# Two semaphores for the dispatched rows of even and odd images, and a wait for the image two back

## What is computed

```
x = x + mixer(ln(x))
t = ln(x) as 8192 tokens
logits = t @ gate_w + gate_b
choice = the best (layer 0) or the two best (layers 1 to 3) of the experts
y = sum over the chosen experts e of  weight[e] * expert_e(t)
x = x + y
```

## Time and profile before

| what | value |
|---|---|
| median of 3 runs | 2364.84 us (2357.2 to 2367.01) |
| profiled execution: its own time, its span | 2363.5 us, 2361.8 us |
| busy share of the span | TensorE 74%, VectorE 66%, ScalarE 50%, GpSimd 42% |
| GpSimd's returns (line 1212) | 488 of 987 ns, 481.8 us busy |
| GpSimd's sends (line 795) | 448, about 0.96 us each, 445.0 us busy |
| DMA | 153.81 MB, 65 GB/s on average |
| granted clock of TensorE | 0.87 of full speed on average |

### The profile page before, as it was taken

How to read it: one execution, slowest core, us unless ns; L and a number is a source line. 1 busy time by engine, 2 the same in 40 slices (tenths; PEclk the granted TensorE clock), 3 DMA queues, 4 the chain that set the end, 5 groups by cost and what they waited for, 6 DMA issues and landing times. The chain is left out here.

```text
span 2361.8 us, 46309 instructions
## 1 busy us (share of the span) xinstructions
PE 1751.2 (74%) x10964; PEld 1380.4 (58%) x10981; DVE 1549.3 (66%) x4683; ACT 1176.6 (50%) x2637; POOL 980.9 (42%) x969
## 2 busy tenths in 40 slices
PE   1488665895388887989971477779918999988992
PEld 1133554895243443989971244657717777687992
DVE  6898686676677777635537677645665677754554
ACT  2445774895233332757752233446726444454661
POOL 0000133453004343655544066677740255466662
PEclk9799666998699999999995687789959999999996
DMA  2002002222201011232223112133343010123326
GB/s 73 1 0 69 16 25 55 55 77 88 82 2 35 22 33 54 64 85 69 68 75 115 36 46 75 60 89 104 90 142 109 19 34 31 50 70 97 92 78 218
DMA packets 183551, 153.81 MB, mean 65 GB/s; under 512 B 40290, under 2 KB 162818, under 8 KB 183358
## 3 DMA queue, kind: packets, MB, share of 16 engines
q1 hardware_dynamic: 153406, 92.37, 14.5%
q0 software_dynamic: 29952, 59.26, 7.4%
HBM read 85.33 MB, written 68.79 MB: 65 GB/s over the span
## 5 line engine op out<-in xcount | busy, mean ns | idle before, releaser
L1212 POOL DMA_INDIRECT returned<-rows_second_choice x488 | 481.8, 987 | 329.5 <-DVE rows_second_choice L1143 119.3
L1011 PE MATMUL psum<-rows_first_choice 128*128 128x128 f32 x3360 | 473.2, 282 | 19.1 <-ACT rows_first_choice L1060 14.7
L1021 PE MATMUL psum<-expert_weights,rows_first_choice 128*128 x2784 | 428.3, 290 | 61.6 <-ACT rows_first_choice L1077 21.8
L1011 PEld LDWEIGHTS psum<-rows_first_choice 128*128 128x128 f32 x3360 | 431.8, 199 | 21.1 <-issue 15.1
L1021 PEld LDWEIGHTS psum<-expert_weights,rows_first_choice 128*128 128x128 f32 x2784 | 362.8, 198 | 99.2 <-issue 93.0
L795 POOL DMA_INDIRECT dispatched<-rows_first_choice,slot x192 | 191.6, 998 | 525.2 <-DVE rows_second_choice L695 375.9
L1077 ACT ACTIVATE rows_first_choice<-psum,bias_columns 128x128 f32<-128x128 f32 x1104 | 323.4, 368 | 171.4 <-PE psum L1011 154.3
L795 POOL DMA_INDIRECT dispatched<-rows_second_choice,slot x192 | 191.5, 998 | 58.5 <-issue 58.2
L1118 DVE COPY rows_first_choice<-expert_weights 128x512 f32 (+1 forms) x272 | 105.5, 388 | 147.4 <-PE psum L1011 122.1
L326 PE MATMUL psum<-identity,rows_first_choice 128*128 128x128 f32 x256 | 41.2, 320 | 202.8 <-DVE rows_first_choice L313 190.8
L1143 DVE SCALAR_TENSOR_TENSOR rows_second_choice<-psum,rows_second_choice,rows_first_choice 128x128 f32<-128x128 f32 x344 | 119.4, 347 | 103.4 <-PE psum L1021 101.3
(11 more groups left out here) (369 smaller groups left out, 3272.9 us busy)
## 6 DMA issues: line engine op xcount, KB each, us to landing
rows_second_choice<-dispatched SPq DMA_DIRECT2D x488, 65.0 KB
expert_weights<-returned SPq DMA_DIRECT2D x12, 1024.0 KB, 10.4
rows_second_choice<-returned SPq DMA_DIRECT2D x8, 1024.0 KB, 10.7
returned<-rows_second_choice POOLq DMA_INDIRECT x488
expert_weights<-in_L_ffn_w SPq DMA_DIRECT2D x3, 2048.0 KB, 8.3
residual<-in_x SPq DMA_DIRECT2D x8, 512.0 KB, 7.2
rows_first_choice<-returned SPq DMA_DIRECT2D x4, 1024.0 KB, 8.9
out<-residual SPq DMA_DIRECT2D x8, 512.0 KB, 6.0
```

The source lines that it names most:

```text
L1011: ins = pe.matmul(k.ps[:, self.PSH + u % 2, j * P:(j + 1) * P], self.wc[:, u % 2, j * P:(j + 1) * P], self.xt[:, u % 2, :], start=True, st ...
L1021: ins = pe.matmul(self.result_bank(u), self.gs[:, u % self.HB, j * P:(j + 1) * P], self.second[:, bass.ds(e, 1), j, :].rearrange("p a c -> ...
L1212: pool.indirect_dma_start(out=k.returned[0:N * self.K, :], out_offset=bass.IndirectOffsetOnAxis(ap=self.rt[:, u, C:C + 1].bitcast(I32), ax ...
```

## The change

The one semaphore `rows_sent` becomes two, `even_sent` and `odd_sent`, by the number of the image. `sent(images, parity)` gives the count at which the images of one parity among the first `images` have been sent. The wait behind the sends of an image is gone. In its place GpSimd waits, ahead of the sends of image b from image 2 on, until image b-2 has landed, in the expert stage too, ahead of image 7. VectorE waits for the same image as before; SyncE waits for both semaphores.

```diff
@@ class Router
+    def sent(self, images, parity):
+
+        return self.when(("even_sent", "odd_sent")[parity], 16 * TPB * self.K * ((images + 1 - parity) // 2))
+
+    def all_sent(self, eng, images):
+        for parity in range(2):
+            eng.wait_ge(*self.sent(images, parity))
@@ place
             if b >= 2:
-                dve.wait_ge(*self.when("rows_sent", 16 * TPB * K * (b - 1)))
+                dve.wait_ge(*self.sent(b - 1, b % 2))
@@ send_tile
-                in_=self.rows[c][:, b * TPB + t, :], in_offset=None).then_inc(self.s["rows_sent"].h, 16)
+                in_=self.rows[c][:, b * TPB + t, :],
+                in_offset=None).then_inc(self.s[("even_sent", "odd_sent")[b % 2]].h, 16)
@@ send
         self.slots_known(pool, b)
+        if b >= 2:
+            pool.wait_ge(*self.sent(b - 1, b % 2))
         for t in range(TPB):
             self.send_tile(pool, b, t)
-        pool.wait_ge(*self.when("rows_sent", 16 * TPB * self.K * (b + 1)))
@@ Experts.sync
-        sp.wait_ge(*route.when("rows_sent", 16 * TPB * self.K * route.first_images))
+        route.all_sent(sp, route.first_images)
...
-        sp.wait_ge(*route.when("rows_sent", 16 * TPB * self.K * B))
+        route.all_sent(sp, B)
@@ Experts.gpsimd
             if t == start:
                 route.slots_known(pool, B - 1)
+                pool.wait_ge(*route.sent(B - 2, (B - 1) % 2))
```

4 lines of the change are left out of this document (2 added, 2 removed).

## The result

| | median, us | lowest to highest | runs |
|---|---|---|---|
| before | 2363.63 | 2357.20 to 2367.01 | 4 |
| changed | 2348.64 | 2347.60 to 2350.73 | 4 |

The profiled execution took 2347.68 us. The result has therefore two parts to explain: some 8 us that can be placed in the traces, where 7.0 were forecast, and a rest of 3 to 6 us that two of the four groups show and two do not.

What follows compares the result with a forecast made beforehand. GpSimd was taken as the slowest link of the spline mixer and pace-setter of its experts. 5.67 + 1.80 - 0.48 gave a 7.0 us lead, passed on whole: 2364.84 - 7.0 = 2357.8 us, range 2350 to 2365.

Steps and rivals of the forecast that it cites:

- What bounds the kernel: Spline layer: GpSimd is the slowest link in the mixer and sets the pace of the experts behind it.
- Image 6 starts when its addresses are there: Spline mixer: image 6's first send starts 0.30 us after its addresses, at 1488.26 instead of 1493.93, 5.67 us earlier.
- The landing of image 6: Spline layer: the first return no longer waits for this landing; 2.10 us becomes 0.30, a gain of 1.80 us.
- One collision of 0.48 us: Spline mixer: one send beside VectorE's wide work takes 0.48 us longer, cutting the lead from 7.47 to 7.0 us.
- The gap behind the first return: Start of the spline experts: counted in 4.3 us of idle time for two gaps at the start; no gain forecast from it.
- The lead passes through the experts: Spline experts: the whole 7.0 us reaches the last return, with bounds of 4.6 and 9.9 us.
- Two semaphores cost nothing: Elsewhere in the kernel: SyncE's and VectorE's waits on two semaphores in place of one change nothing.
- The other layers: Involution and attention first returns start 1.8 us earlier, but waits for results use this up: nothing, at most 3.6 us.
- More than forecast: Rival: GpSimd's 2.9 us of waits for results vanish and other layers keep 3.6 us, giving 2351.3 us; chance 0.12.
- Given back by the clock: Rival: spline experts' tiles at TensorE's lower clock cost 0.6 us each; twelve undo the gain, 2364.8 us; chance 0.16.
- it does not do what it says: Rival: something untraced ties addresses and landings, so the next image still starts late, giving 2364.8 us; chance 0.05.
- Slower: Rival: 24 more spline expert tiles at the lower clock cost 14 us, less the 7.0, giving 2372 us; chance 0.05.

Runs made afterwards that it cites:

- spline_only: Changed kernel with the new waits in the spline layer alone, old waits in the other three layers, two semaphores: 2354.69 us, ratio to before 0.9975.
- not_spline: Changed kernel with the old waits in the spline layer and the new ones in the other three, two semaphores: 2359.08 us, ratio to before 0.9999.
- long_sync: Changed kernel with each of SyncE's waits for the rows sent written three times in the fractal layer: 2348.02 us, ratio to before 0.9951.
- hold_again: Changed kernel with the wait for image 6's own landing kept behind its sends: 2351.93 us, ratio to before 0.9968.
- lean: Changed kernel with another semaphore saved in the fractal mixer's loads, so as many as before: 2642.89 us on a slower chip, ratio to before there 1.0037.

## Why the prediction was right or wrong

**What bounds the kernel: right.** 10 us of the gain are in the spline layer and come with its own waits, as the traces of spline_only and not_spline show.

**Image 6 starts when its addresses are there: right.** 5.67 us predicted, 5.65 measured. That the sends of images 1 to 5 leave nothing over was argued from one sum (1486 against 1487.96), and it holds, by less than the sum says: images 4 and 5 wait 1.9 and 1.7 us for addresses of their own, and image 6's first send stands 0.47 us behind the end of image 5's last, only 0.17 more than the usual gap. That the new wait never comes last has a simpler reason than the 20 us of sends: VectorE waits for the same landing before it writes the addresses that GpSimd needs.

**The landing of image 6: right.** 1.80 predicted, 1.81 measured.

**One collision of 0.48 us: mis-sized.** Image 1's first send takes 1.22 us now, 0.26 over the 0.96 of others, and image 6's takes 0.96. The collisions of images 1 to 5 lie ahead of addresses that are waited for and cost nothing, and image 6's did not occur. The term is nothing, and the lead at the first return is 7.46 us, not 7.0. The 2.5 us worked out from the Trainium skill (SBUF — State Buffer, section "A bandwidth-pool intuition that's wrong (but worth ruling out)") did not come about: image 1's first send, beside three wide operations of VectorE that take 2.07 us together, took 1.44 us before and 1.22 after, and not 3.1. That page's price is for a copy whose size it does not give; whether a send is held until the single operation beside it ends, as it also says, these rows do not decide.

**The gap behind the first return: missed.** This is the step that failed first. The prediction knew the gap (it took it off the 47.4 us as "the two gaps at the start", 4.3 us) and treated the second, 2.19 us, as something that stays. It was bound to the wait that was removed: 1.89 us. With it, the 0.48 above and 0.8 that came behind it, the spline layer gives 10.1 us and not 7.0. The "issue" behind an idle time was read as a fixed cost of the instruction; its neighbours at 0.30 said that it was none.

**The lead passes through the experts: right.** 9.35 us at the second return are 10.1 at the last, by the means of four traces; the 0.8 us between them are less than the last stretch scatters. TensorE's waits for rows are shorter, and its clock in the catch-up is higher, not lower (0.76 to 0.88 against 0.56 to 0.63, above).

**Two semaphores cost nothing: wrong.** This is the second step that failed, and its sign is the other one: they cost 1.86 us at the end of the fractal experts. The prediction looked at who waits for them, and there is no wait in the profile that names them.

**The other layers: right in sum, as far as the traces tell.** Their leads are lost before the last return. In the attention mixer the way to image 6's first send is 0.5 us shorter (194.38 to 193.88, the same in all four traces of either kernel to 0.03), but the whole layer takes 454.8 us before and 454.6 after, the means of four: nothing of it is left. The involution layer's experts end as long behind image 6's first send as before (293.0 and 293.2), with the open point told under spline_only.

The corrected sum is -10.1 + 1.9 = -8.2 us. The 22 runs of the changed kernel on two chips give -8.7 and -7.3. That the forecast 7.0 is close to this is in part luck: it left out 3.1 us of gain and 1.9 of loss, and the two have opposite signs. The spans of the four traces of either kernel differ by more, 2358.9 and 2347.9 in the mean, 11.0 us; the 2.8 us beyond the sum lie spread over the fractal and involution layers and their borders, where single traces of one kernel differ by as much.

The time that the prediction gave, 2357.8, was measured from a median of three runs of before, 2364.84, which is 5 to 6 us above the two medians of 35 runs (and 2.5 above the one of 19), while the changed kernel's later medians, 2351.35 and 2351.97, lie inside the range. The four runs behind 2348.64 lie below them by 3 us. So of the miss of 9.2 us about 1.2 is the sum's (8.2 for 7.0), some 5 are the median that it was taken from, and 3 the four runs of the changed kernel. Whether the last two are chance is open: long_sync, in a later group, has 2348.02 us in four runs too, beside 2362.36 for before.

**The rivals.** "More than forecast" came nearest in its number (2351.3) and not in its mechanism: it wanted the leads of the other layers, which are lost, and all of the waits for results. "Given back by the clock" and "it does not do what it says" fall. "Slower" has no place in the traces of the chips of 2360 us; on those of 2630 the variants are slower, by a way that is not found.

## What to carry to other kernels

A wait that blocks an engine's program costs more than its idle time: what the program has to prepare between the wait and the next instruction (here a register) comes on top, and shows as an odd gap put down to "issue", so compare each such gap with its neighbours before you call it fixed. "Issue" can also hide a plain wait for another engine: of the waits for addresses, seven changed their name between the two traces and hardly their length. A lead is worth its full size only where the engine that has it is the slowest link of the stage, and whether it is can change from one chip to the next. For effects of a few us, marks in one engine's timeline over several traces say more than medians of four runs; but a mark that the whole time does not follow, as in hold_again, is half a proof.

## What the runs showed of the hardware

- Two chips of the five ran the same kernel in 2630 us where the others need 2360. Their profiled executions have a granted clock of 0.844 to 0.851 against 0.869 to 0.874. In lean, beside the changed kernel's first trace, GpSimd is busy for as long (978.1 and 977.2 us), VectorE too (1545.8 and 1547.0), TensorE for 71 us more (1820.9 and 1749.4) of the 287 us that the span is longer; the rest is waiting, up to 14.5 us before an image's logits. What causes it was not found.
- Setting a register between a wait for a landing and a DMA of GpSimd's puts 1.6 us between that DMA and the next (3.19 us with it, 1.58 with the register set ahead). Where nothing blocks, in the changed kernel, the figure is 1.30.
- Counting GpSimd's DMAs on two semaphores in place of one made one barrier of four 1.86 us later (6.88 and 8.74 us from the last return to the first load behind it), the one figure in five traces, the other in fifteen.
- Eight memsets of 512 columns on GpSimd took 3.80 us.
